# A transformer block on one core: its twelve looped turns written out, and the order of TensorE's two programs exchanged

## What is computed

```python
x = x + attn_a(layernorm(x), Wq, bq, Wk, bk, Wv, bv, Wo, bo)   # 16 heads of 16; window of 32 each way, 4 global tokens
x = x + ffn(layernorm(x), w_gate, w_up, w_down)                # 256 -> 768 -> 256, int32 weights times 1/127
x = x + attn_b(layernorm(x), Wqkv, Wout, bout)                 # rotary, causal numerator, unmasked denominator
x = x + ffn(layernorm(x), w_gate, w_up, w_down)

def ffn(x, w_gate, w_up, w_down):
    return (silu(x @ wg.T) * (x @ wu.T)) @ wd.T
```

## Time and profile before

| | us |
|---|---|
| median of three runs | 2593.28 |
| lowest, highest | 2589.51, 2595.23 |
| the profiled execution | 2595.68 |
| its span, from the first to the last instruction | 2593.9 |

### The profile page before, as it was taken

How to read it: one execution, slowest core, us unless ns; L and a number is a source line. 1 busy time by engine, 2 the same in 40 slices (tenths; PEclk the granted TensorE clock), 3 DMA queues, 4 the chain that set the end, 5 groups by cost and what they waited for, 6 DMA issues and landing times.

```text
span 2593.9 us, 70330 instructions
## 1 busy us (share of the span) xinstructions
PE 2095.5 (81%) x25221; PEld 1439.7 (56%) x25221; DVE 1402.5 (54%) x2972; ACT 1448.9 (56%) x3580; POOL 814.4 (31%) x1131
## 2 busy tenths in 40 slices
PE   3567888889797888979798797979889797978775
PEld 2355455656564665656465565646556574645444
DVE  3355446564655657465565646556474655645433
ACT  1214656657475655747565674756567475755572
POOL 0013133333333323243323333332333333333321
PEclk7668789989898999989899998989999898988887
DMA  4222324151432415143241414234242423323121
GB/s 144 49 70 69 76 74 86 55 120 51 104 71 79 88 59 111 51 108 67 85 85 61 106 51 112 67 88 83 67 94 62 103 69 96 73 76 70 55 57 37
DMA packets 129727, 202.82 MB, mean 78 GB/s; under 512 B 26768, under 2 KB 60560, under 8 KB 129312
## 3 DMA queue, kind: packets, MB, share of 16 engines
q1 hardware_dynamic: 129344, 197.80, 31.8%
HBM read 67.87 MB, written 51.52 MB: 46 GB/s over the span
## 4 chain that ended last, share of the span: by engine, by line
PE 51%; issue 19%; DVE 9%; ACT 9%; DMA 5%; POOL 4%; SPq 2%; ACTq 1%; DVEq 0%; POOLq 0%
PE gu_bank L1007 15%; PE d_bank L1023 7%; ACT s_bank L1134 5%; PE o_bank L939 5%; PE s_bank L902 3%; PE gu_bank L982 3%; PE gu_bank L1035 3%; PE s_bank L889 3%; PE s_bank L769 3%; PE s_bank L923 2%; DMA xn<-o_scr_B 2%; PE s_bank L882 2%; ACT probs_B L1124 2%; PE s_bank L777 2%; SPq L522 1%
## 5 line engine op out<-in xcount | busy, mean ns | idle before, releaser
L1134 ACT ACTIVATE s_bank<-s_bank 128x512 f32<-128x512 f32 x1024 | 605.2, 592 | 217.5 <-PE s_bank L902 216.8
L1555 POOL TENSOR_TENSOR h<-tmp,h 128x512 fp32r<-128x512 f32 x192 | 246.4, 1284 | 622.9 <-DVE h L1419 620.2
L1124 ACT ACTIVATE probs_B<-s_bank 128x512 f32<-128x512 f32 x640 | 341.7, 601 | 170.4 <-PE s_bank L923 160.7
L1401 DVE SCALAR_TENSOR_TENSOR tmp<-tmp,gu_bank 128x512 f32<-128x512 f32 x192 | 131.6, 686 | 361.6 <-ACT tmp L1163 361.6
L1572 POOL TENSOR_SCALAR_AFFINE_SELECT probs_B<-probs_B 128x256 f32<-128x256 f32 x512 | 200.8, 422 | 199.1 <-ACT probs_B L1124 199.1
L902 PE MATMUL s_bank<-pack_b 48*128 48x512 f16 x1024 | 206.4, 409 | 55.5 <-ACT s_bank L1134 41.3
L1007 PE MATMUL gu_bank<-xT,w_g 128*128 128x256 f32 x1536 | 238.0, 294 | 8.1 <-DVE tmp L1401 4.1
L1023 PE MATMUL d_bank<-w_d,h 128*128 128x256 f32 x1536 | 230.9, 292 | 6.4 <-POOL h L1555 6.0
L1007 PE MATMUL gu_bank<-xT,w_u 128*128 128x256 f32 x1536 | 234.2, 291 | 0.4 <-DVE tmp L1407 0.4
L1007 PEld LDWEIGHTS gu_bank<-xT,w_g 128*128 128x128 f32 x1536 | 197.2, 189 | 41.4 <-issue 17.0
L1023 PEld LDWEIGHTS d_bank<-w_d,h 128*128 128x128 f32 x1536 | 194.2, 188 | 43.1 <-issue 30.6
(11 more groups left out here) (144 smaller groups left out, 3491.1 us busy)
## 6 DMA issues: line engine op xcount, KB each, us to landing
pack_b<-src_b SPq DMA_DIRECT2D x768, 64.0 KB, 2.5
pack_a<-src_a SPq DMA_DIRECT2D x384, 64.0 KB, 2.3
x<-in_L_attn_a_x_dram SPq DMA_DIRECT2D x32, 512.0 KB, 4.2
o_scr_A<-o_raw SPq DMA_DIRECT2D x64, 256.0 KB, 2.0
o_scr_B<-o_raw SPq DMA_DIRECT2D x64, 256.0 KB, 2.7
rden_on<-r_scr_A SPq DMA_DIRECT2D x32, 256.0 KB
xn<-o_scr_A SPq DMA_DIRECT2D x32, 256.0 KB
x_scr<-x SPq DMA_DIRECT2D x16, 512.0 KB, 2.6
```

Source lines behind the costliest of these rows:

```text
L1124: act.activation(probs["B"][:, n % RING, :], score_bank(s, "N", n // 2, n % 2)[:, :], ACT.Exp, scale=SM_SCALE)\
L1134: act.activation(bank[:, :], bank[:, :], ACT.Exp, scale=SM_SCALE, accum_out=den[:, 0, j, 2 * tile + e, t:t + 1]).then_inc(den_exp, 1)
L1555: pool.tensor_tensor(h[1][:, i % 2, :], tmp[:, i % 2, :], h[0][:, i % 2, :].bitcast(F32), ALU.subtract)\
```

## The change

The three parts become one list of 20 slots, `all_slots = [Slot(k, 0) for k in range(-1, SEQS + 3)]`, which each engine walks with `turn` = 0. No hardware loop is left, and every wait compares with a constant. On PE the condition of the `If` is turned round, so that `slots(True)` stands first and `slots(False)` in the `Else`. The steps, their order in a slot, the buffers, the transfers and the arithmetic are the same.

```diff
--- before.py
+++ after.py
@@ -61,7 +61,6 @@
 LNS, FS, OS, PS = ("F2", "F1", "PB", "NA"), ("F2", "F1"), ("OB", "OA"), ("PA", "PB")
 GU = {"VB": 2, "RB": 4, "PA": 6, "VA": 2, "OB": 2, "OA": 2, "F2": 2 + 2 * FT, "F1": 2 + 2 * FT, "PB": 6}
 DU = {"F2": 2, "F1": 2}
-FIRST, STEADY = 3, 12
 
 
 
@@ -259,9 +258,7 @@
 def build(nc, x_in, Wq, bq, Wk, bk, Wv, bv, Wo, bo, Wqkv, Wout, bout, w_gate, w_up, w_down,
           cos_in, sin_in, masks_in, eye_in, sel_in, swap_in, strip_in, a_fill_in, v_fill_in, out):
     nc.disable_value_cache = True
-    before_loop = [Slot(k, 0) for k in range(-1, FIRST)]
-    body = Slot(FIRST, 1)
-    after_loop = [Slot(k, 0) for k in range(FIRST + STEADY, SEQS + 3)]
+    all_slots = [Slot(k, 0) for k in range(-1, SEQS + 3)]
     v_scr = nc.dram_tensor("v_scr", (HEADS * GLOBALS, HEADS, DH + 1), F32).ap()
     o_scr = {b: nc.dram_tensor(f"o_scr_{b}", (GROUPS, P, S), F32).ap() for b in "AB"}
     r_scr = {b: nc.dram_tensor(f"r_scr_{b}", (GROUPS * 4, S), F32).ap() for b in "AB"}
@@ -675,11 +672,7 @@
                         sp.dma_start(x1[:, :, :], x_in[bass.ds(s.seq["OA"].at(turn), 1)].rearrange("a (t p) n -> p (a t) n", p=P))\
                             .then_inc(x1_in, 16)
 
-            for s in before_loop:
-                slot(s, 0)
-            with sp.Fori(0, STEADY) as turn:
-                slot(body, turn)
-            for s in after_loop:
+            for s in all_slots:
                 slot(s, 0)
             sp.wait_ge(x_stored, 16 * SEQS)
 
@@ -1082,17 +1075,13 @@
                         swap_step(s, n, turn)
 
             def slots(exact):
-                for s in before_loop:
+                for s in all_slots:
                     slot(s, 0, exact)
-                with pe.Fori(0, STEADY) as turn:
-                    slot(body, turn, exact)
-                for s in after_loop:
-                    slot(s, 0, exact)
-
-            with pe.If(is_general > 0):
+
+            with pe.If(is_general < 1):
+                slots(True)
+            with pe.Else():
                 slots(False)
-            with pe.Else():
-                slots(True)
 
 
         @block.scalar
@@ -1222,11 +1211,7 @@
                     act.activation(st_dT[:, f:f + 2, :], bank.rearrange("p (k n) -> p k n", k=2), ACT.Copy).then_inc(w_staged, 1)
             act.wait_ge(c_in, 16 * NC)
             act.wait_ge(w_raw, 48)
-            for s in before_loop:
-                slot(s, 0)
-            with act.Fori(0, STEADY) as turn:
-                slot(body, turn)
-            for s in after_loop:
+            for s in all_slots:
                 slot(s, 0)
 
 
@@ -1512,14 +1497,10 @@
                     elif kind == "VC":
                         v_taken(s, block, n, turn)
 
-            for s in before_loop:
+            for s in all_slots:
                 slot(s, 0)
                 if s.k == -1:
                     split_b()
-            with dve.Fori(0, STEADY) as turn:
-                slot(body, turn)
-            for s in after_loop:
-                slot(s, 0)
 
 
         @block.gpsimd
@@ -1610,11 +1591,7 @@
                     elif kind == "W2":
                         rotate(s, n, turn)
 
-            for s in before_loop:
-                slot(s, 0)
-            with pool.Fori(0, STEADY) as turn:
-                slot(body, turn)
-            for s in after_loop:
+            for s in all_slots:
                 slot(s, 0)
```

## The result

The changed kernel takes 2549.4 us in the median of four runs (2545.4 to 2550.7), against 2593.8 for the kernel before (2589.5 to 2595.2). The ratio is 0.9829, with a 95% interval of 0.9812 to 0.9846: 44 us less, where 39 were forecast (2554, range 2534 to 2566). The profiled execution took 2549.7 us, its span is 2547.9.

A forecast was written before the change was run, and what follows sets the result against it. PE's stream was taken to set the pace, stalled by eleven taken branches. Twelve turns of 112.6 + 34.1 = 146.7 us make 1760.4 against 1799.5, 39.1 less: 2556.6 profiled, 2554 for the median, range 2534 to 2566.

The forecast's parts named there:

- The stall at eleven boundaries: PE's loop end: removing eleven taken branches brings turns to 146.7 us, 39.1 us less over slots 3 to 14.
- The entry: From a slot's L1043 to its L796: 34.1 us expected in every turn, with ends of 32.45 and 34.88.
- Register steps: Register steps ahead of waits, on all engines: their removal takes 0.1 us off the mean entry, nothing from L796 on.
- The branches of the other engines at 0: Loop ends of DVE, ACT and POOL: gain 0, since DVE's lasts 63 ns and each has over 40% idle time.
- The order of the programs at 0: PE's branch at the start, 4.73 us, becomes a fall-through: gain 0, hidden by the first layer norm.
- The jump at the end: PE's jump over the other program, ending between 2592.3 and 2593.3: cost 0, bounds 0 and 0.6 us.
- The short entry: Rival: all entries 32.45 us like slot 4's, turn 145.1, gain 58.8 us, median 2534.5; chance 12%.
- The late load of straight code: Rival: written-out bodies' instruction loads come late, costing 90 us; kernel 51 us slower, 2644; chance 4%.
- The 108 ns: Skill's price per compare-and-branch: eleven make an estimated 1.2 us, so no change; the trace's 3754 ns on PE contradicted it.

The follow-up runs named there:

- e3: Kernel before with only PE's program written out and its program branch turned; DVE, ACT, POOL and SP keep their loops: 2559.3 us.
- e5: Changed kernel with eleven taken branches put back on PE behind slots 3 to 13, over 2 to 1024 never executed matmuls: 2568.0 us, one execution.
- e11: Changed kernel with SP issuing the last store o_scr_B<-o_raw of a sequence ahead of the two loads of the reciprocals: 2549.3 us.
- e4: Kernel before with DVE, ACT, POOL and SP written out; PE keeps its loop and the old order of its branch: 2593.4 us.
- e10: Kernel before with PE, DVE and SP written out and PE's program branch turned; ACT and POOL keep their loops: 2554.2 us.
- e9: Kernel before with PE and DVE written out and PE's program branch turned; ACT, POOL and SP keep their loops: 2563.9 us.
- e1: Changed kernel, all turns written out, but PE's two programs in the old order, so PE jumps at the start: 2552.0 us.
- e2: Kernel before, loop kept, but PE's integer-weight program first in its branch, so PE falls through at the start: 2588.5 us.
- e8: Kernel before with a loop of six turns of two slots on every engine, so five taken branches in place of eleven: 2587.5 us.
- e12: Changed kernel with SP's store ahead of the reciprocal loads and the load xn<-o_scr_B ahead of six pack_b transfers: 2539.3 us.
- e6: Kernel before with 32 never executed matmuls behind PE's float32 program, so that later code moves: 2585.4 us.
- e7: Kernel before with 96 never executed matmuls behind PE's float32 program, so that later code moves: 2627.2 us.

## Why the prediction was right, and where not

**The stall at eleven boundaries** was the right mechanism at the right size. Forecast was a turn of 146.7 us, measured 146.8; 39.1 us forecast, 37.7 measured, 3.4 for each taken branch. e3 and e5 show it from both sides: writing out PE alone gives 27.0 of the 37.7 us in these slots, and each far branch put back costs 3.3. No gap is left at a boundary and the V product takes 3.09 us. Rows of the one turn without a taken branch were enough to price it.

**The entry** was forecast at 34.1 us from the three slots with a fast V product; measured, it is 33.4 to 34.3. The size is right and the reason is half of it. The text laid the difference between 32.45 and 34.1 on the clock and the rotary chain. For slot 6 this holds: its clock was 0.76, and slots 12 and 14 of e5 have the long entry at 0.75 with the load on time. What the text left out is SP's queue. The late PE had given SP 3.7 us of lead, and with PE on time the chain runs through SP's store and load. Slots 3 and 15 of the kernel before had shown it already: SP starts 0.3 and 0.6 us behind the swap there, the load goes out at 11.7 and 12.1, and DVE waits 2.1 and 2.2 us for it. e11 shows that the load is not all of it either. How the 1.6 us divide between the two was not measured.

**Register steps**: a gain of 0.1 us a turn was taken off. e4 and e10 show nothing of it in the time, and the reading was a weak one: in slot 3 of the kernel before, with register steps, `PA`'s first product starts 9.34 us after the swap, sooner than in slot 15 without them. PE's own register steps were never tried by themselves.

**The branches of the other engines at 0** was right for the change, which removes them. But the reason, that they have idle time, does not hold. With PE written out and the others looping, slots 3 to 14 take 10.7 us more, and e9 against e10 lays a loss of this size on SP. Busy shares don't tell that an engine is idle at the moment when it is waited for.

**The order of the programs at 0** was right for the branch itself: PE's first transposes start at 53.40 us, 53.16 before, and wait for DVE. It missed the 9.4 us ahead of slot 3 in the profiled pair. They go with a low clock and with gaps in slot 0's value products, which the profile marks "issue" and which are read as late instruction loads here (no run shows the loads themselves). The kernels without such gaps mostly reach slot 3 later where the clock over the window shown above is lower: between 360.2 and 361.7 us at 0.83 (the changed kernel, e1, e2, e8), between 362.3 and 363.6 at 0.70 to 0.76 (e3, e5, e9, e12), at 365.2 and 367.0 at 0.63 (e11, e6), and at 364.7 at 0.57 (e10). Those with gaps reach it at 371.1 at 0.57 (before), 368.2 at 0.63 (e4) and 366.8 at 0.76 (e7). By e10 the clock alone is 3.0 of the 9.4 us and the gaps are the other 6.4, by one execution each. The gaps were seen only in kernels that jump at the start, but e1, e6 and e8 jump and have none. The clock does not follow the order of the programs: e10 has the new order. So the 9.4 us are in part those of the two executions, and by the medians of e1 and e2 the order gives 2.6 to 4.2 us. The total came 5 us under the forecast because of this term and not because of the loop; that it stayed inside the forecast's own range of 2549 to 2559 is in part luck.

**The jump at the end** is as forecast (the source view counts two branches on this line, the short one at the start and this jump; the forecast spoke of one):

```profile
L1081 PEldq COMPARE_BRANCH  x2: 86/2004/3922, 46.1 to 2542.3; - x2
...
2544.28 0.39 SPq L650 DMA_DIRECT2D out_dram<-x  x1
```

It ends at 2546.2, the span at 2547.9, so the last store covers it.

**The rivals.** The short entry did not come in the changed kernel; e5 has it again in three of the slots where PE is late. The late load of straight code did not come: between slot 3 and slot 15 PE has one gap marked "issue" of over 0.3 us, where the kernel before has 32.6 us of them, and instruction loads on the queue fell from 230 to 202. The 108 ns that the Trainium skill gives for a compare-and-branch ("Advanced Engine Details and Errata", "Control Flow Timing") lie between this case's 83 ns for one that is not taken and 207 to 353 ns for a near one; they do not describe the far one of 3.3 us and more. The Trainium skill's rule ("Runtime: NRT & Kernel Launch", "Instruction fetch mechanics") is that a taken branch whose target is not in the loaded code has to wait for a load. e5 agrees with it: at most 353 ns over up to 128 matmuls, at least 3300 ns over 256 and more.

## What to carry to other kernels

Read the source view of the loop's branch: its longest and shortest duration, and the one turn in which it is not taken, price the loop before anything is built. When a stall is removed from the leading engine, look at the engines that used its lateness as a head start, here the in-order DMA queue of SP, and take their loop ends out together with it. Two kernels with a far jump can differ by over 1% by where their code lies, so a small difference between them says little.

## What was not expected of the hardware

- A taken branch on PE lasted 0.21 to 0.35 us over up to 128 matmuls and 3.3 to 3.9 us over 256 and more (e5).
- 96 matmuls that never run moved the time from 2593 to 2627 us, 32 of them to 2585.
- On DVE and SP the branch shows as 63 ns or less, and the engine's next work still came 0.6 to 0.9 us late.
- A shorter wait does not have to make a shorter turn. In e11 PE waits less, its granted clock is lower, and the turn stays at 146.8. Three pairs of slots in e8 (4 and 5, 6 and 7, 8 and 9) take 300.2 to 300.3 us, twice the usual 150.2 of the kernel before, though it has half the branches. Other lengths do occur (143.5 to 147.8 in e12); why these values was not settled.
